# Attention over 16 narrow heads: key and query copies laid out in blocks of 16 partitions instead of interleaved every sixth

## The reference

```python
q = split_heads(queries @ Wq.T)          # 16 heads of HD = 16
k = split_heads(keys @ Wk.T)
v = split_heads(values @ Wv.T)
scale = 1.0 / jnp.sqrt(jnp.asarray(HD, q.dtype))
scores = jnp.einsum('bhqd,bhkd->bhqk', q, k) * scale
attn = jax.nn.softmax(scores, axis=-1)
ctx = jnp.einsum('bhqk,bhkd->bhqd', attn, v)
...
return out @ Wo.T
```

## Time and profile before

| what | value |
|---|---|
| median of 3 runs | 871.25 us (867.67 to 878.57) |
| the profiled execution's own time | 871.25 us |
| its span | 869.6 us |
| granted TensorE clock, mean of the span | 0.978 |

### The profile page before, as it was taken

The page is one execution under the profiler, slowest core; times in us unless marked ns, Lnnn a source line. Parts: engine busy times, 40 slices in busy tenths (PEclk is TensorE's granted clock), DMA queues, the critical chain, the costliest instruction groups (busy, mean ns, idle before and its releaser), DMA issues. The chain is left out here.

```text
span 869.6 us, 14271 instructions
## 1 busy us (share of the span) xinstructions
PE 783.0 (90%) x5120; PEld 512.1 (59%) x5120; DVE 475.6 (55%) x1100; ACT 262.5 (30%) x522; POOL 279.1 (32%) x295
## 2 busy tenths in 40 slices
PE   5987999889999979989999999999888888998985
PEld 4664657555765545556665665665665556665764
DVE  2447474246633656714343554636677866778632
ACT  1223211241123121112222222231245544445450
POOL 4573515050410322601612525445952220101011
PEclk9999999999999999999999999999999999999997
DMA  8786835422350292834676555665856643842000
GB/s 211 215 269 210 221 99 153 143 88 71 112 147 0 99 373 96 271 99 141 192 199 194 180 163 169 192 202 172 240 159 176 177 133 119 207 115 57 23 24 21
DMA packets 70014, 133.34 MB, mean 153 GB/s; under 512 B 9797, under 2 KB 50758, under 8 KB 68026
## 3 DMA queue, kind: packets, MB, share of 16 engines
q1 hardware_dynamic: 54312, 81.02, 30.2%
q10 hardware_dynamic: 7794, 31.15, 13.1%
q0 software_dynamic: 7840, 20.26, 8.7%
HBM read 103.92 MB, written 28.31 MB: 152 GB/s over the span
## 5 line engine op out<-in xcount | busy, mean ns | idle before, releaser
L1558 DVE TENSOR_REDUCE mxh<-ps 112x2 f32<-112x750 f32 x128 | 114.9, 934 | 37.5 <-PE ps L1860 37.0
L1272 PE MATMUL ps<-rw,rowsT 128*128 x280 | 130.6, 609 | 1.7 <-ACT rowsT L1233 0.9
L1732 ACT ACTIVATE d_pT<-ps 125x448 f32<-125x448 f32 x192 | 90.8, 549 | 74.6 <-PE ps L1880 68.5
L988 PE MATMUL ps<-x1T,sw 128*128 128x448 f32 x256 | 102.8, 547 | 6.1 <-DVE gluT L459 4.1
L1272 PEld LDWEIGHTS ps<-rw,rowsT 128*128 128x128 f32 x280 | 50.9, 192 | 59.2 <-issue 59.2
L988 PEld LDWEIGHTS ps<-x1T,sw 128*128 128x128 f32 x256 | 46.8, 190 | 51.7 <-issue 39.2
L1860 PE MATMUL ps<-kst,qst 96*112 96x375 bf16 x256 | 65.2, 344 | 11.5 <-DVE mxh L1558 6.7
L1289 PE MATMUL ps<-rw,gT 128*128 x280 | 66.4, 380 | 0.8 <-ACT gT L1237 0.8
L1289 PEld LDWEIGHTS ps<-rw,gT 128*128 128x128 f32 x280 | 52.9, 190 | 21.4 <-issue 16.0
L319 POOL DMA_INDIRECT xg<-xh_moe,places x32 | 33.0, 1032 | 88.4 <-DVE places L546 51.6
L999 PE MATMUL ps<-sw,gluT 128*112 128x256 f32 x256 | 57.6, 380 | 2.9 <-DVE gluT L459 1.4
(11 more groups left out here) (222 smaller groups left out, 1257.8 us busy)
## 6 DMA issues: line engine op xcount, KB each, us to landing
rb<-in_rb SPq DMA_DIRECT2D x35, 512.0 KB
kst<-kscr ACTq DMA_DIRECT2D x45, 378.0 KB, 5.4
rw<-in_rw SPq DMA_DIRECT2D x24, 512.0 KB
kscr<-ka SPq DMA_DIRECT2D x16, 567.0 KB, 3.5
cT<-in_ctx_t SPq DMA_DIRECT2D x21, 378.0 KB, 9.6
ctxT<-in_ctx_t SPq DMA_DIRECT2D x16, 378.0 KB
ctxn<-in_ctx SPq DMA_DIRECT2D x16, 375.0 KB
qst<-qscr ACTq DMA_DIRECT2D x12, 448.0 KB, 8.0
```

The lines of the kernel that those rows point to most:

```text
L988: last = mm(bank[up_in(i, m)[k]][:, 0:GS], w[:, e, c, h * P:(h + 1) * P], x1T[:, c, :], start=c == 0, stop=c == C - 1)
L1272: last = mm(bank[1 + 2 * q + k], rowsT[:, q, c * P:(c + 1) * P], w[:, e, c, :], start=c == 0, stop=c == C - 1)
L1558: V.tensor_reduce(mxh[:, 2 * g:2 * g + 2], ps[0:S, 2 * (g % 2):2 * (g % 2) + 2, 0:K], axis=AX_X, op=ALU.max).then_inc(s["s_max"], 1)
L1732: A(pT[:, q % 2, k, :], bank[4 + k][0:KC, 0:QUAD * S], ACT.Exp).then_inc(s["p_ready"], 1)
```

## The change

The 96 partitions of `kst` and `qst` are laid out in six blocks of 16: copy r of feature d is now at partition 16r + d. The order of the products along the contraction changes with it, and both operands change alike. Keys still come in three DMAs, now of 48, 32 and 16 adjacent partitions (parts 0 to 2, parts 0 and 1, part 0). Queries come in six DMAs of 16 adjacent partitions each in place of three of 32; none has a broadcast source. PE's wait for the queries counts six DMAs in place of three. The three parts stand in another order in `qa`; the instructions that compute them are the same in number, engine and shape.

```diff
-        return s[f"qs_in{i % 2}"], (i // 2 + 1) * 3 * 16
+        return s[f"qs_in{i % 2}"], (i // 2 + 1) * 6 * 16
...
-    def load_key_copies(eng, b, a):
-        eng.dma_start(kst[b % 4][a:DEPTH:3, :, :].rearrange("p h t -> p (h t)"),
-                      kscr[b].rearrange("s (d g) x -> d s (g x)", d=HD)[:, 0:3:2 if a == 2 else 1, :][:, 0:2, :]).then_inc(s[f"k_in{b % 4}"], 16)
+    def load_key_copies(eng, b, part):
+        first_copy, n = ((0, 3), (3, 2), (5, 1))[part]
+        eng.dma_start(kst[b % 4][first_copy * HD:(first_copy + n) * HD, :, :].rearrange("p h t -> p (h t)"),
+                      kscr[b].rearrange("s (d g) x -> (s d) (g x)", d=HD)[0:n * HD, :]).then_inc(s[f"k_in{b % 4}"], 16)
...
-        eng.tensor_copy(qa[:, 1, :, :], qr[:]).then_inc(s["q2_ready"], 1)
+        eng.tensor_copy(qa[:, 0, :, :], qr[:]).then_inc(s["q2_ready"], 1)
...
-        eng.tensor_tensor(qa[:, 0, :, :], qr[:], qa[:, 2, :, :], ALU.subtract).then_inc(s["q3_ready"], 1)
+        eng.tensor_tensor(qa[:, 2, :, :], qr[:], qa[:, 1, :, :], ALU.subtract).then_inc(s["q3_ready"], 1)
...
     def load_queries(a, i):
         a.wait_ge(s["q_out"], (i + 1) * 16)
-        parts = qscr[i].rearrange("s (d g) x -> d s (g x)", d=HD)
-        for r in range(3):
-            two = parts[:, 0:2, :] if r == 2 else parts[:, r + 1:r + 2, :].to_broadcast([HD, 2, NH * GS])
-            a.dma_start(qst[i % 2][r:DEPTH:3, :, :].rearrange("p h t -> p (h t)"), two).then_inc(s[f"qs_in{i % 2}"], 16)
+        for r, k in enumerate((0, 0, 0, 1, 1, 2)):
+            a.dma_start(qst[i % 2][r * HD:(r + 1) * HD, :, :].rearrange("p h t -> p (h t)"),
+                        qscr[i, k].rearrange("(d g) x -> d (g x)", d=HD)).then_inc(s[f"qs_in{i % 2}"], 16)
```

More of the change, by code:

```diff
@@ L1354, in queries_in @@
         i = b // G
-        return s[f"qs_in{i % 2}"], (i // 2 + 1) * 3 * 16
+        return s[f"qs_in{i % 2}"], (i // 2 + 1) * 6 * 16
     def late_load(b):
         return B + b - NV
-    def load_key_copies(eng, b, a):
-        eng.dma_start(kst[b % 4][a:DEPTH:3, :, :].rearrange("p h t -> p (h t)"),
-                      kscr[b].rearrange("s (d g) x -> d s (g x)", d=HD)[:, 0:3:2 if a == 2 else 1, :][:, 0:2, :]).then_inc(s[f"k_in{b % 4}"], 16)
+    def load_key_copies(eng, b, part):
+        first_copy, n = ((0, 3), (3, 2), (5, 1))[part]
+        eng.dma_start(kst[b % 4][first_copy * HD:(first_copy + n) * HD, :, :].rearrange("p h t -> p (h t)"),
+                      kscr[b].rearrange("s (d g) x -> (s d) (g x)", d=HD)[0:n * HD, :]).then_inc(s[f"k_in{b % 4}"], 16)
     def load_keys(eng, b):
-        for a in range(3):
-            load_key_copies(eng, b, a)
+        for part in range(3):
+            load_key_copies(eng, b, part)
     def load_context(eng, b):
@@ L1387, in split_queries @@
             eng.wait_ge(s["q_out"], i * 16)
-        eng.tensor_copy(qa[:, 1, :, :], qr[:]).then_inc(s["q2_ready"], 1)
+        eng.tensor_copy(qa[:, 0, :, :], qr[:]).then_inc(s["q2_ready"], 1)
         eng.wait_ge(s["q2_ready"], 3 * i + 1)
-        eng.tensor_tensor(qr[:], qr[:], qa[:, 1, :, :], ALU.subtract).then_inc(s["q2_ready"], 1)
+        eng.tensor_tensor(qr[:], qr[:], qa[:, 0, :, :], ALU.subtract).then_inc(s["q2_ready"], 1)
     def split_rest(eng, i):
         eng.wait_ge(s["q2_ready"], 3 * i + 2)
-        eng.tensor_copy(qa[:, 2, :, :], qr[:]).then_inc(s["q2_ready"], 1)
+        eng.tensor_copy(qa[:, 1, :, :], qr[:]).then_inc(s["q2_ready"], 1)
         eng.wait_ge(s["q2_ready"], 3 * i + 3)
-        eng.tensor_tensor(qa[:, 0, :, :], qr[:], qa[:, 2, :, :], ALU.subtract).then_inc(s["q3_ready"], 1)
+        eng.tensor_tensor(qa[:, 2, :, :], qr[:], qa[:, 1, :, :], ALU.subtract).then_inc(s["q3_ready"], 1)
         eng.wait_ge(s["q3_ready"], i + 1)
```

## The result

The changed kernel takes 915.57 us in the median of 4 runs (913.06 to 917.13), the kernel before 871.43; the profiled execution took 912.1 us, span 910.4. Over all 16 executions on record the changed kernel took 902.17 to 919.10 us; the ratio, from which its slow ones are left out, is 1.0426 with a 95% interval of 1.0363 to 1.0491, some 37 us. That is slower, and outside the range given (866 to 893).

A forecast was written before the change was run, and what follows sets the result against it. The prediction took PE, busy 783.0 of 869.6 us, as the bound. It added 3.7 + 1.8 + 1.4 + 1.0 = 7.9 us to 871.25 for 879 us, range 866 to 893.

The forecast's parts named there:

- The forecast's first step: Query loads: a row takes 1.9 us in place of 0.95, a group 11.5 us in place of 5.7.
- no more than a third more: Key loads: they take at most a third longer, since 48, 32 and 16 partitions average 32, as before.
- Who waits behind them: SP's maxima DMAs take turns with slower query rows, so six packets take 1.5 times as long; sum with clock 7.9 us.
- Block 4 into 5: Maxima rows before block 5: 7.5 us become 11.2, so PE, already waiting, waits 3.7 us longer.
- before block 9: Maxima rows from block 8 into 9: 6.5 us become 9.8, less 1.8 us of slack; 1.8 us taken.
- Before the attention: SP's queue empties later, against 3.3 us of slack before PE is due: between 0.4 and 2.4, taken as 1.4 us.
- Beside the experts: Group 0's query load, issued at 561.7 and read at 608.5 while PE is fully busy: cost 0.
- The clock: A new wait before block 9 may bring a half-clock stretch of PE: at most 1.5 us, taken as 1.0.
- The keys at 0: Key loads, first read 18 us after issue, cost nothing by themselves, even if their time doubled.
- Rival 2: Load rate falls with partitions addressed: 47 GB/s, 930 us; milder form, three times a row's time, 892 to 895; chance 0.12.
- Rival 1: Load rate is kept and finer interleaving ends PE's wait before block 5: 868 us, or 871 without effect; chance 0.32.
- Rival 3: ACT's added query issues block, delaying exponentials in blocks 4 and 8: 878 us, or 885 with maxima's delay; chance 0.10.

The follow-up runs named there:

- q_six_striped: Kernel before with six query DMAs without broadcast, each to every sixth partition, keys as before: 869.82 us, ratio 0.9991.
- queries_blocks: Kernel before with only the query loads changed, to six DMAs of 16 adjacent partitions: 900.05 us, ratio 1.0351.
- keys_blocks: Kernel before with only the key loads changed, to 48, 32 and 16 adjacent partitions: 883.69 us, ratio 1.0142.
- group_0: q_six_striped with only group 0's queries, loaded beside the experts, on 16 adjacent partitions a DMA: 877.57 us, ratio 1.0076 to the kernel before.
- rates: Loads alone, without computation, in eleven ways: 96 rows take 7.8 us to every third partition, 8.3 to every sixth, 12.5 as six blocks of 16.
- pairs_32: Kernel before with the same key and query DMAs written to 32 adjacent partitions in place of every third one: 887.70 us, ratio 1.0182.

## Why the prediction was wrong

**The rate was right in size, for a wrong reason.** The forecast's first step, a query row in 1.9 us and 120 GB/s with full engines, is what the trace shows (120 and 119), and the query loads land in 11.6 us in the median, as said. But I had doubled the row's time because a DMA now addresses 16 partitions in place of 32, and q_six_striped, whose DMAs address 16 as well, loses nothing. What counts is that they are adjacent. That the doubling fitted is luck. The keys' "no more than a third more" is 9.5 against 6.7 us, 42%. Six issues cost PE nothing, as said; each is even shorter, 442 ns in the median against 609.

**"Who waits behind them" failed, in four terms.** Of this step's list:

- *Block 4 into 5: 3.7 longer.* It was 7.6 (9.33 against 1.72), and before block 9 5.2 where I said 1.8. From the issue of the maxima DMAs to PE's start it takes 10.2 us in the kernel before; the forecast makes that 13.9, and it was 17.8. The step scaled the time in which SP's packets take turns with ACT's, and had finer interleaving win a quarter of it back. It left out that the time before the first of them is served would grow too: 2.7 us after issue in the kernel before, 7.6 here. SP issued the maxima DMAs of block 5 at 713.82; this is 719 to 722, then 722 to 725:

```profile
q10 hardware_dynamic: 59, 0.30, 91.4%
q1 hardware_dynamic: 4, 0.00, 0.3%
...
q10 hardware_dynamic: 69, 0.37, 104.7%
q1 hardware_dynamic: 56, 0.01, 5.6%
```

  Four of 96 packets are served in the first 8 us after issue, the last seven after 728. Here they mostly wait for what lies queued ahead, some 45 of the 96 query rows among it, and only then take turns. In block 8 it is the other way round: the first are served 3.7 us after issue and the last near 797, so the turns alone take over 10 us, against some 7 in the kernel before. How the engines choose is not settled by these runs.
- *Before the attention: 1.4.* It was 13.9. I compared SP's queue with one deadline, that of the maxima rows. The same queue carries the context loads, with deadlines of their own: PE waited 2.54 and 5.06 us for them. The maxima rows were late as well. Their last DMA landed 25.2 us after issue, the longest of all that touch the query tile, and that is the 4.17 us before the first transposed scores:

```profile
DMA to landing us min/median/max: 1.7/7.1/25.2
```

  queries_blocks and keys_blocks alone cost 8.3 and 3.3 us there, 11.6 of the 13.9.
- *Beside the experts: 0.* It was a 4.04 us wait and the slow stretch behind it, 7.5 us in the trace; group_0 measures 0.8% of the time. I had argued from PE's 7.00 busy of 7.00 us, which says what PE did, not how soon the next tile's rows had to land. The row to read was the landing time of those rows against their tile.
- *The clock: 1.0.* PE's busy time rose by 12.3 us. I charged one new wait; from the experts to the end of the attention there were seven of over 2 us (4.04, 2.54, 5.06, 4.17, 2.34, 9.33 and 5.20) where the kernel before has one (2.88, before the attention), each with a stretch at the lower level behind it, of 3.4 to 13.7 us.

**The keys at 0.** PE indeed never waits for keys, as I said, but slower keys fill the same engines under values, context and maxima: 12 to 13 us alone, two thirds of it as PE's longer busy time. "These loads by themselves cost nothing" was true of their own arrival and wrong as a price.

**The rivals.** Rival 2's mild form (892 to 895) was nearest in size, yet its mechanism, the rate in proportion to the partitions a DMA addresses, is refuted by q_six_striped. Rival 1 is refuted by the rate; its half about interleaving may hold for q_six_striped, where the wait before block 5 is 0.37 us, but no time comes of it. Rival 3 is refuted: the exponentials behind the six issues start 0.7 us after their scores, where 0.4 is usual. The figure that the Trainium skill gives in the section named above (104 GB/s for 16 adjacent partitions) agrees with the 120 measured in the kernel, and with the 110 of the six blocks in rates (1.376 MB in 12.5 us), in direction and nearly in size; it was the step behind it that made 885 of it in place of 915.

## What to carry to other kernels

Look at which partitions a DMA writes: the same 96 rows took 12.5 us as six DMAs of 16 adjacent partitions and 8.3 as six on every sixth, and with rows twice as long a step of two was as good as one of eight. When a large transfer gets slower, its own consumer may have all the slack in the world; list every other transfer that is in flight beside it on any queue, with the time by which each is needed, the small ones first. A wait of PE costs its length and, where the clock falls, part of the work behind it: here 28.5 us of new idle time came with 12.3 us of longer busy time. And when a cure removes one wait, add up all of PE's waits again before you believe it.

## What the runs showed of the hardware that I had not expected

- Small DMAs of one queue wait for large rows of another queue even though both are served by all 16 engines: three DMAs of 3.5 KB land 4.6 us after issue beside striped rows, 8.1 beside adjacent ones, and 9.5 beside rows that touch none of their partitions' neighbours. With nothing else running, beside six blocks, two large rows an engine start first, and then as many small rows as large ones.
- A query DMA is issued in 442 ns in the median in the changed kernel and 609 in the one before. Adjacent partitions alone don't do it (pairs_32: 610), nor does the plain source alone (q_six_striped: 611); it takes both.
- Steps of two, four and eight partitions are equally fast (15.5, 15.3, 15.4 us for 2.75 MB, step one 25.0); step two is enough, and eight is not better.
- PE's busy time rose by 12.3 us, for the same matmuls, in a kernel in which it idled 28.5 us more: the granted clock falls to 0.50 while PE waits and stays there for some us of work (until 737.8, 6 us after the 9.33 us wait had ended).
